# A fused linear-attention and mixture-of-experts block: gathers moved ahead of the loop, attention added to the output in three groups, and two projections reordered

## The reference

```python
x = L0_attn_x
xn = _layernorm(x, axis=-1)
x = x + _L0_attn_ref(xn, ...) + _L0_ffn_ref(xn, ...)

# attention: q and k are the same projection, no softmax over tokens
q = x @ Wqk + bqk
v = jax.nn.silu(x @ Wv + bv)
u = jax.nn.silu(x @ Wu + bu)
kv = jnp.einsum('bhnd,bhne->bhde', elu(heads(q)), heads(v))   # 16 heads of 16
out = jnp.einsum('bhnd,bhde->bhne', elu(heads(q)), kv)
out = (u * _layernorm(out, ln_g, ln_b)) @ Wo + bo

# experts: 8, the 2 best of each token
probs = jax.nn.softmax(xt @ gate_w.T)
expert_weights, expert_indices = jax.lax.top_k(probs, 2)
h = jax.nn.silu(xt @ w1[e].T) * (xt @ w3[e].T)                 # 512 wide
out = sum of expert_weights * (h @ w2[e].T) over the two experts
```

## Time and profile before

| | |
|---|---|
| median of 3 executions | 304.72 us (304.63 to 308.46) |
| the profiled execution | 301.63 us, span 299.9 us |
| mean granted TensorE clock | 0.950 |
| busy: PE, PEld, DVE, ACT, POOL | 242.4, 158.6, 189.9, 152.0, 135.3 us |
| DMA | 50.48 MB, mean 168 GB/s |

### The profile page before, as it was taken

The page is one execution under the profiler, slowest core; times in us unless marked ns, Lnnn a source line. Parts: engine busy times, 40 slices in busy tenths (PEclk is TensorE's granted clock), DMA queues, the critical chain, the costliest instruction groups (busy, mean ns, idle before and its releaser), DMA issues.

```text
span 299.9 us, 6061 instructions
## 1 busy us (share of the span) xinstructions
PE 242.4 (81%) x1784; PEld 158.6 (53%) x1784; DVE 189.9 (63%) x413; ACT 152.0 (51%) x255; POOL 135.3 (45%) x128
## 2 busy tenths in 40 slices
PE   0327998996678886999999999999999979989400
PEld 0117776874455443576666666666566545555200
DVE  3998799499874798685859586867674323333000
ACT  2876784186568661736374545455564323434100
POOL 6375000173300005667874672747265564316561
PEclk9999799999977997999999999999999999999765
DMA  6999992088935339999999999899989999797552
GB/s 209 412 420 407 424 427 107 0 212 237 183 59 76 59 78 119 139 177 146 170 170 130 153 210 127 119 138 178 181 107 152 147 172 124 132 150 109 82 58 32
DMA packets 86290, 50.48 MB, mean 168 GB/s; under 512 B 72547, under 2 KB 83811, under 8 KB 85061
## 3 DMA queue, kind: packets, MB, share of 16 engines
q1 hardware_dynamic: 76516, 35.42, 52.7%
q0 software_dynamic: 9744, 14.69, 32.1%
HBM read 23.35 MB, written 11.67 MB: 117 GB/s over the span
## 4 chain that ended last, share of the span: by engine, by line
PE 29%; DMA 13%; DVE 9%; issue 8%; POOLq 6%; ACT 5%; POOL 1%; ACTq 0%; DVEq 0%
PE bank L1144 16%; PE bank L1157 8%; DMA out<-regions,row_out 5%; POOLq L452 5%; DMA out<-xn 4%; DVE regions L748 3%; ACT regions L527 3%; PE bank L1196 3%; DMA xrow<-xrow 2%; DMA out<-area,row_out 2%; DVE xrow L940 2%; PE bank L1173 1%; PE bank L1185 1%; POOL out L461 1%; DVE xrow L945 1%
## 5 line engine op out<-in xcount | busy, mean ns | idle before, releaser
L1144 PE MATMUL bank<-regions,xg_all 128*128 x468 | 108.9, 384 | 3.9 <-DMA xg_all<-regions 2.1
L1144 PEld LDWEIGHTS bank<-regions,xg_all 128*128 128x128 f16 x468 | 44.6, 99 | 54.7 <-issue 8.2
L1157 PE MATMUL bank<-regions,xrow 128*128 x468 | 59.7, 280 | 7.5 <-DMA xrow<-xrow 7.4
L1157 PEld LDWEIGHTS bank<-regions,xrow 128*128 128x128 f16 x468 | 46.1, 100 | 21.7 <-issue 10.6
L613 ACT ACTIVATE xrow<-xrow 128x512 f16<-128x512 f32 x39 | 24.6, 630 | 58.5 <-DVE xrow L940 58.5
L940 DVE SCALAR_TENSOR_TENSOR xrow<-bank,xrow 128x512 f32<-128x512 f32 x39 | 26.9, 691 | 38.4 <-PE bank L1144 35.2
L461 POOL DMA_INDIRECT out<-area,row_out x20 | 33.6, 1680 | 30.9 <-issue 13.3
L461 POOL DMA_INDIRECT out<-regions,row_out x19 | 31.2, 1643 | 28.7 <-issue 17.5
L439 POOL DMA_INDIRECT xrow<-xsplit,row_in x8 | 11.3, 1408 | 66.4 <-DMA xg_all<-xrow 33.4
L945 DVE TENSOR_TENSOR xrow<-xrow 128x512 f16<-128x512 f32 x39 | 26.9, 690 | 21.6 <-ACT xrow L613 21.6
L608 ACT ACTIVATE xrow<-bank 128x512 f32<-128x512 f32 x39 | 23.2, 595 | 27.7 <-PE bank L1144 27.5
(11 more groups left out here) (150 smaller groups left out, 304.1 us busy)
## 6 DMA issues: line engine op xcount, KB each, us to landing
regions<-wexp SPq DMA_DIRECT2D x8, 1536.0 KB, 13.9
xsplit<-xrow SPq DMA_DIRECT2D x4, 512.0 KB, 9.6
out<-xn POOLq DMA_DIRECT2D x8, 256.0 KB
area<-x SPq DMA_DIRECT2D x2, 768.0 KB, 7.7
regions<-wattn SPq DMA_DIRECT2D x1, 1032.0 KB, 10.6
xrow<-xrow SPq DMA_TRANSPOSE x39
area<-x SPq DMA_DIRECT2D x1, 512.0 KB, 3.5
regions<-xsplit,row_in POOLq DMA_INDIRECT x31, 4.7
```

The costliest lines, as they stand in the source:

```text
L1144: last = mm(bank_[:], xg[t % 4][:, KD * d + k, :], w16[:, bass.ds(e, 1), w, at:at + I].rearrange("p a c -> p (a c)"), start=(k == 0 and n ...
L1157: last = mm(ps_y[t % 2][:, 0:D], hT[t % 2][:, IC * d + c, :], w16[:, bass.ds(e, 1), w, at:at + D].rearrange("p a c -> p (a c)"), start=(c ...
```

## The change

It does five things.

1. **More gathers in the front.** Twelve gather buffers are laid into a second weight region, which the front frees. So `gather(4)` to `gather(15)` are issued by POOL right after the copy of x, waiting only for the second expert's low half (`w_lo` 2); gathers 16 to 19 go at t = 8 to 11, the rest with the attention groups.
2. **Loads.** Experts are loaded in the order 0, 2, 3, 4, 1, 5, 6, 7 into other regions; expert 1 takes the place of the attention weights after their split, expert 7 that of expert 0 after its split.
3. **Experts.** Experts 0 to 3 are split whole in the front, experts 4 to 7 in halves of 1536 columns (`hi_half`, `expert_lo_half`): the first half at the end of the front, the others behind tiles 0, 1, 2, 3 and 5 of the loop (one, two, one, two and one).
4. **Order in the front.** `invert()` goes ahead of the third pair's projections; `v_proj(p+2)` goes behind `kv(p)`; `k_lo(0)` goes ahead of `expert_lo(0)`, `halves(1)` ahead of `exps(2)`, and the experts' splits move between the pairs.
5. **Attention in three groups.** Pairs 0 to 2, 3 to 5 and 6 to 7 are added at t = 13, 22 and 28, each group with two gathers ahead of its wait.

```diff
-EARLY = 5
+EARLY = 4
+HALVES_AT = ((1,), (2, 3), (4,), (5, 6), (), (7,))
+HALF = WCOLS // 2
+RAW = (E, E + 1) + tuple(range(3, E)) + (E,)
 FEW = 4
-PLACES = 16
+MANY = 12
+MORE = 8
+PLACES = FEW + MANY + MORE
 PAIR_AT = [4 + 3 * p for p in range(NP)]
-FIN_AFTER = {PAIR_AT[2 * i + 1] + 4: (2 * i, 2 * i + 2) for i in range(NP // 2)}
+GROUPS = {PAIR_AT[2] + 3: (0, 3, 20, 28), PAIR_AT[5] + 3: (3, 6, 28, 36), PAIR_AT[7] + 3: (6, 8, 36, ST)}
...
             load_expert(0)
+            load_expert(2)
+            store_split(0)
+            load_expert(3)
+            store_split(1)
+            load_expert(4)
+            store_split(2)
+            sp.wait_ge(attn_lo, 1 + KD)
             load_expert(1)
-            for c in range(TT // CH):
-                store_split(c)
-                load_expert(2 + c)
-            load_expert(E - 2)
-            sp.wait_ge(attn_lo, 1 + KD)
-            load_expert(E - 1)
+            store_split(3)
+            load_expert(5)
+            load_expert(6)
+            sp.wait_ge(w_lo, 1)
+            load_expert(7)
...
             def gather(t):
-                if FEW <= t < 2 * FEW:
-                    pool.wait_ge(xg_loaded[t % 4], 16)
-                if t == 2 * FEW:
-                    pool.wait_ge(w_lo, E)
-                if t >= 2 * FEW + PLACES:
-                    pool.wait_ge(xg_loaded[t % 4], 16 * ((t - PLACES) // 4 + 1))
+                if t == FEW:
+                    pool.wait_ge(w_lo, 2)
+                if t == FEW + MANY:
+                    pool.wait_ge(late_lo, 2 * (E - EARLY))
+                if t >= PLACES:
+                    done = t - PLACES + FEW
+                    pool.wait_ge(xg_loaded[done % 4], 16 * (done // 4 + 1))
...
-            for t in range(FEW, 2 * FEW):
+            for t in range(FEW, FEW + MANY):
                 gather(t)
...
-            def add_attention(p0, p1, n):
-
+            def add_attention(n, p0, p1, t0, t1):
+
+                for t in range(t0, t0 + 2):
+                    gather(t)
                 for i in range(2):
                     pool.wait_ge(y_added[i], 16 * (1 + (n + 1 - i) // 2))
                 for p in range(p0, p1):
                     pool.wait_ge(fin_ready, p + 1)
                     g.dma_start(out_pairs[:, p, :, :], fin(p).rearrange("p (j d) -> p j d", d=D),
                                 accum_op=ALU.add).then_inc(fin_added, 16)
-                for t in range(2 * FEW + PLACES + 3 * p0, min(ST, 2 * FEW + PLACES + 3 * p1)):
+                for t in range(t0 + 2, t1):
                     gather(t)
                 pool.wait_ge(fin_added, 16 * p1)
...
+            def hi_half(n):
+                e, part = EARLY + n // 2, slice(HALF * (n % 2), HALF * (n % 2 + 1))
+                if n == 0:
+                    act.wait_ge(w_lo, EARLY)
+                elif n % 2 == 0:
+                    act.wait_ge(late_lo, n)
+                act.wait_ge(raw_loaded[e], 16)
+                a.activation(w16[:, e, 0, part], raw(e)[:, part], ACT.Copy, scale=SCALE).then_inc(late_hi, 1)
...
             exps(1)
+            halves(1)
             exps(2)
-            halves(1)
-            act.wait_ge(w_lo, 1)
+            act.wait_ge(w_lo, 2)
             hi(2)
             exps(3)
             halves(2)
-            act.wait_ge(w_lo, 2)
-            hi(3)
             exps(4)
             halves(3)
+            act.wait_ge(w_lo, 3)
+            hi(3)
             exps(5)
+            halves(4)
+            exps(6)
             kv_halves(0)
-            halves(4)
-            act.wait_ge(w_lo, 3)
-            hi(4)
-            exps(6)
             halves(5)
             exps(7)
             halves(6)
             halves(7)
+            hi_half(0)
             a.activation(warm[:], log_scale[:], ACT.Silu).then_inc(warm_done, 1)
             kv_halves(1)
...
             for t in range(ST + 2):
-                if t < E - EARLY:
-                    act.wait_ge(w_lo, EARLY - 1 + t)
-                    hi(EARLY + t)
...
                 if t < ST:
                     h_hi(t)
+                if t < len(HALVES_AT):
+                    for n in HALVES_AT[t]:
+                        hi_half(n)
...
-            kv_proj(1)
+            k_proj(1)
+            v_proj(1)
+            invert()
             for p in range(NP):
                 if p + 2 < NP:
-                    kv_proj(p + 2)
-                if p == 0:
-                    invert()
+                    k_proj(p + 2)
                 kv(p)
+                if p + 2 < NP:
+                    v_proj(p + 2)
```

More of the change, by code:

```diff
@@ L477, in _ @@
             for t in range(ST):
[L478 to L482 removed]
+                if t in GROUPS:
+                    add_attention(t, *GROUPS[t])
+                if 8 <= t < 12:
+                    gather(t + 8)
                 add_expert(t)
@@ L910, in _ @@
             row_tables()
-            k_lo(0)
+            expert_lo(1)
             maps(2)
@@ L1005, in _ @@
                     finish(phase(t, 3))
-                if t < E - EARLY:
-                    expert_lo(EARLY + t)
+                if t < len(HALVES_AT):
+                    for n in HALVES_AT[t]:
+                        expert_lo_half(n)
         @block.tensor
```

47 lines of the change are left out of this document (26 added, 21 removed).

## The result

The changed kernel took **312.75 us** (median of 4 runs, 312.17 to 317.22) and the kernel before, run beside it, 304.68: a ratio of 1.029, 95% interval 1.0196 to 1.0384. It is slower, by 2% to 4%. The forecast was 298.4 with a range to 304.8, so both sign and range were wrong. The profiled execution took 312.24 (span 310.5, mean granted clock 0.945; before 301.63, 299.9, 0.950), 10.6 more than before. Some executions of any kernel here are slower as a whole, with a lower clock: ratios compare the others, and as the profiled executions of e1, e6 and e9 are of the slower kind, only their stretches are read and not their totals.

A forecast was written before the change was run, and what follows sets the result against it. It took POOL's add queue to bound the end, PE the middle and DVE the loop's start. Terms -7.5 - 1.8 + 3.0 = -6.3 put the profiled execution at 295.3 and the median at 298.4 us, range 293.5 to 304.8.

The forecast's parts named there:

- `row_in`: Front: with three products' worth of PE work moved behind it, it comes 2.4 us earlier, at 55.2.
- The copy moves with it: Front: first four gathers and copy of x shift 2.4 us earlier; copy issued at 61.9, landed at 72.8.
- The k transpose: Front, gating `halves(4)`: sharing evenly with eight queued gathers after the copy, it ends at 80.4 against 80.0 before.
- Rival 2: Front: DMA queues share by packets, not time, so the transpose of k lands at 82.9; 300.9 us, chance 0.14.
- rival 4: Front: twelve gathers keep the transpose of k until all have landed, 88.9; slower than before, 306.9 us, chance 0.09.
- `halves(4)` to `h_mul(0)`: End of the front: the new order shortens this stretch from 18.3 to 16.8 us.
- Tiles 0 to 3: Loop's start, `h_mul(0)` to `center`: DVE waits for ACT's halves, 22.8 us in place of 17.8, a loss of 5.0.
- 0.9 given back by the gathers that leave the loop: Loop's start: without gathers beside it, the transpose of tile 4 takes 4.5 us in place of 5.36.
- The full stretch stays so: Middle of the loop: PE's full stretch starts 3.0 us late and keeps that delay.
- POOL stops being the bound: Kernel's end: POOL's queue of adds no longer delays the last add, which follows PE's own end; gain 7.5 us.
- the sign of being wrong that I had named: Kernel's end: the forecast is wrong if POOL's last adds still run back to back; no size given.
- One group less: Loop between 235 and 275 us: one attention group's DMAs there instead of two save PE transpose waits, 1.8 us.

The follow-up runs named there:

- e1: Changed kernel with the twelve early gathers held back on POOL until the first two transposes of k have landed: 307.63 us, ratio 1.0111.
- e6: Changed kernel with the copy of x issued ahead of the wait for `row_in` and attention in four groups: 305.67 us, ratio 1.0091.
- e9: Changed kernel with expert 1's low half moved behind the expert tables: 308.68 us, ratio 1.0276.
- e5: Changed kernel with expert 7's load issued behind the second transpose of k: 311.98 us, ratio 1.0354.
- e8: Kernel before with only the change's reordering of inversion, k and v, plus `k_lo(0)` and `halves(1)` moved ahead: 301.51 us, ratio 0.9987.
- e12: e8 with the copy of x issued early, against the kernel before: 301.68 us, ratio 1.0026.
- e14: The same kernel as e8, the reordering alone, run again in five rounds against the kernel before: 300.18 us, ratio 0.9943.
- e13: e8 with the last attention group at t = 28 in place of 29: 298.97 us, ratio 0.987 to the kernel before.
- e2: Changed kernel with the copy of x issued ahead of the wait for `row_in`: 301.23 us, ratio 0.997.
- e10: e2 with the late experts' halves spread one a tile over tiles 0 to 6: 307.52 us, ratio 1.0299.
- e4: Changed kernel with attention added in four groups of two pairs in place of three groups: 313.69 us, ratio 1.0361.
- e7: e6 with expert 7's load late and expert 1 loaded second, into the second region: 302.1 us, ratio 1.0043.
- e11: e10 with four attention groups and expert 1's low half behind the expert tables: 311.0 us, ratio 1.0401.

## Why the prediction was wrong

The steps in order; "shift" is against the kernel before.

- **`row_in`** 2.4 earlier: measured 1.9. Right.
- **The copy moves with it** ("The first four gathers and the copy of x move with it"): wrong. Shift +1.0, not -2.4. I moved POOL's instructions along DVE's without looking at what DVE does beside them: the new order puts a 3.35 us operation right behind `row_in`, and that held the first gather 3 us (e9: 1.22 for 4.33; e5: not the load). The trace of before had shown it, in two gathers that I left out: the one at 66.71 ended 0.90 after DVE's operation, the one at 77.91 ended 0.82 after a later one.

```profile
66.71 2.90 POOL L439 DMA_INDIRECT xrow<-xsplit,row_in  x1 [1.26 <-DMA xg_all<-xrow]
77.91 1.75 POOL L439 DMA_INDIRECT xrow<-xsplit,row_in  x1 [2.09 <-DMA xg_all<-xrow]
```

- **The k transpose** at 80.4: measured 84.7, and here the forecast fell. 2.75 of the 4.3 is the copy, landed at 75.6 and not 72.8. Behind the copy I gave the transposes 4.8 + 2.8 = 7.6, and they took 9.2. That both queues share the time about evenly held from 76 to 80 us (61% and 54%), and then the transposes had more (84% and 36%); the count was off. I priced the eight gathers that would stand in the queue. Four stood in it at 75.6, since POOL had been held three times, and six more were issued before the transpose landed. 4.8 us of transposes, and q0's share of the time behind the copy (0.54 x 4 + 0.36 x 4.5 = 3.8), make 8.6. Rival 2 had put 10.1 behind the copy and rival 4 16.1, so in size rival 2 was nearest, by other means than it named.
- **`halves(4)` to `h_mul(0)`** 16.8: measured 19.35. The new order alone did shorten the stretch in three executions of four (17.7 in e8, e12 and e14, 18.6 in e13). In the changed kernel PE came to it after 10.3 us of idling and worked at 1.2 GHz from 86 to 91. Against e14 the loss lies between `exps(6)` and `exps(7)`, 6.4 us for 3.5, where these projections stand; the rest of the stretch is 1.2 shorter. Rival 4 named the lower clock as a remark and left it unpriced.
- **Tiles 0 to 3** 22.8, a loss of 5.0: measured 22.7, as in all eight kernels with those halves. Right, and DVE's waits for ACT are 0.7 as said.
- **0.9 given back by the gathers that leave the loop**: nothing. From `center` to the fifth `down` 10.9 before and 10.9 after; there PE's wait for DVE and its slow half of a hidden layer stood last, and no transpose. 3.0 late became 10.7.
- **"The full stretch stays so"**: it lost 3.7 more. PE fell behind by 0.8 at t = 16 and by 3.3 at t = 25 and 26, each time a few tiles behind a group of three attention DMAs (waits of 1.52 and 1.39 above). Other traces repeat it: with three groups (changed, e2, e5, e10) PE loses against the kernel before 0.4 to 3.6 us at t = 16 and 17 and 2.4 to 5.2 at t = 25 and 26; with four groups (e4, e7, e11) 0.9 to 2.3 at t = 14 and 15 and 1.0 or 1.1 at 26. So the groups cost PE something three or four tiles later. But D with four groups is 111.8 to 116.2, no shorter, so three at once are not shown to be the cause of the 3.7. That stays open.
- **POOL stops being the bound**, -7.5: measured -5.6, and the sign of being wrong that I had named came true: the last adds still run back to back, and add 28 went at 277.3 and not 257. The queue ran empty only at the last add. The 7.5 was itself a misreading. I took 0.53 us as the time from a `y_out` (241.47) to its add (242.47), but counted in order that add is number 24 and that `y_out` number 28. Measured from the end of its own `y_out` the last add starts 2.3 to 2.7 us later in nine of the ten kernels with early gathers (3.5 in e4), and 8.0 in the kernel before: the queue was worth 5.6 us, and all of it went.
- **One group less**, -1.8: not borne out. PE's stretch from the 28th `down` to the last is 1.7 longer, with waits of 1.86, 2.11 and 2.73 (before, 2.13 and 2.74). But e5, with the same loop, has this stretch at 43.4 us, e2 at 44.1 and e1 at 48.6, against 47.0 here and 45.2 before: one execution does not tell its sign.

Sum: 10.7 + 3.7 - 5.6 + 1.8 = +10.6, for the forecast's 3.0 - 7.5 - 1.8 = -6.3. (The last two measured terms are the least sure: at the end, executions of one kernel differ by 3 us.) Of the 16.9 between them 7.7 lie ahead of the fifth `down`, 3.7 in the middle, 5.5 at the end. Rival 4, at 306.9 and with a chance of 0.09, had the side right and the place: e1 and e2 show that the twelve gathers hold that transpose, with the late copy as a second condition it didn't have. Its extreme, all twelve first, did not come, and with the give-back, the full stretch and the end mis-sized the time still went past it.

Rival 2 said packets are shared in turn and not time. From 76 to 80 us q1 moved 1095 packets and q0 85: not one for one. The Trainium skill's page DMA: Bandwidth & Descriptors, under queues, rings and completion order, says that an engine "drains a whole packet" of several descriptors before it switches; if the trace counts descriptors, its rule is neither confirmed nor refuted here. What the runs show is the share of time, near even at first.

Two things stay open: why PE loses so much more behind the groups in some kernels (of e10's 13.7 us of extra D the late halves explain 5.5, 8.8 lie behind two of its groups, and 0.6 comes back elsewhere), and how e9's A divides between copy and gathers (moving both at once was that run's flaw).

## What to carry to other kernels

When an edit makes one engine earlier, lay out what the other engines do beside it at the new time; an operation that was harmless between two transfers can land on the one that everything waits for. Queued background transfers are priced by all that will be issued until the gated one lands, not by those that stand in the queue when it starts. Where a profile names what ended a wait, count the instructions: here it named an ACT operation of a later tile, and the forecast took the cost of an add from such a pairing. Take a change of several parts to pieces: here the reordering alone gave 0.6%, and 1.3% with the last group one tile earlier, while the early gathers shortened POOL's end by some 5 us and, beside the late copy, cost more than that ahead of the loop.

## What the runs showed of the hardware

- **A gather that starts while DVE runs a long operation with both inputs in SBUF is held until that ends.** In all sixteen kernels 37 gathers started inside the splitting of an expert's low half (3.35 us, f16 from f32), and all 37 ended 0.81 to 1.09 us after it; those that started 0.1 to 0.5 ahead of such an operation took 0.95 to 1.25. Short operations show the difference that the inputs make: of the gathers that started inside `h_lo` (0.69 us, both inputs in SBUF) all 56 ended at least 0.81 after it, the longest taking 1.47; of those inside `h_mul` (0.69 us, one input in PSUM) some ended 0.34 after it, and none took over 1.09. The Trainium skill's page SBUF — State Buffer, under "Who interferes with whom", says that a DVE instruction with two SBUF inputs contends with a GpSimd instruction that reads SBUF, and that the order of issue decides which of the two is blocked. The trace agrees in both. Whether it is the read of the rows' numbers or the writing of descriptors that is held, no run here tells.
- **A transpose beside the copy of x from DRAM to DRAM hardly moves**: 0.9% of the DMA engines from 68 to 75 us against 60.4% for the copy's queue, though its queue held work; in the kernel before, 9.1% against 74.2% from 68 to 74. With the gathers held back, in e1, it had 80.4% from 77 to 82, where the copy's queue still took 13.1%.
- **An add starts no less than 2.0 us after its `y_out` ends**: so in all 624 adds of the sixteen kernels. Adds in a queue start about 2.2 us apart at the end of the changed kernel, as in the earlier trace rows.
